# Attention and mixture-of-experts block on one core: queries and keys projected transposed, heads placed by DMAs

## What is computed

```python
xn = layernorm(x)
# latent branch, 16 heads: 16 content + 64 rotary features each
c_q, c_kv = xn @ w_dq.T, xn @ w_dkv.T
q = concat([heads(c_q @ w_uq.T), rope(heads(c_q @ w_qr.T))])
k = concat([heads(c_kv @ w_uk.T), rope(heads(xn @ w_kr.T))])
v = heads(c_kv @ w_uv.T)
s = softmax(causal(q @ k.T / sqrt(80))) @ v @ w_out.T
# second branch, 16 heads of 16
xr = rmsnorm(xn, w_ln1)
h = softmax(causal((xr @ Wq.T) @ (xr @ Wk.T).T / 4)) @ (xr @ Wv.T)
x2 = xn + h @ Wo.T
g = silu(x2 + top2_of_8_experts(rmsnorm(x2, w_ln2)))
out = x + s * g
```

## Time and profile before

| | us |
|---|---|
| median of three runs | 896.05 |
| the profiled execution's own time | 900.06 |
| its span, first to last instruction | 898.3 |
| TensorE matmul busy | 822.7 (92%) |
| VectorE busy | 612.4 (68%) |
| ScalarE busy | 502.1 (56%) |
| GpSimd busy | 391.4 (44%) |
| mean granted TensorE clock | 0.945 |

### The profile page before, as it was taken

One profiled execution on the slowest core, in us unless ns is written; L12 is line 12 of the kernel. 1 busy time (PEld: TensorE's weight loads), 2 busy tenths in 40 slices (PEclk: granted clock), 3 DMA queues, 4 the chain that ended last, 5 costly groups with the idle time before them and its releaser, 6 DMA issues.

```text
span 898.3 us, 18344 instructions
## 1 busy us (share of the span) xinstructions
PE 822.7 (92%) x6432; PEld 735.3 (82%) x6432; DVE 612.4 (68%) x2191; ACT 502.1 (56%) x1089; POOL 391.4 (44%) x538
## 2 busy tenths in 40 slices
PE   5889999999999999999999999988669999999980
PEld 3778988898897898888889889866459999999980
DVE  4976666767767676667776675762537878887854
ACT  2445466457347536536645744644237878787851
POOL 4632342344344344434434434414344565656640
PEclk9988999999999999999999999977769999999995
DMA  9000000000000000000000000122368999999836
GB/s 291 2 1 2 14 1 12 16 13 3 25 14 2 25 14 1 26 13 2 14 14 13 3 25 13 11 87 86 105 183 207 237 230 232 255 261 243 234 37 198
DMA packets 49871, 71.07 MB, mean 79 GB/s; under 512 B 12067, under 2 KB 36003, under 8 KB 49763
## 3 DMA queue, kind: packets, MB, share of 16 engines
q1 hardware_dynamic: 39060, 57.41, 20.8%
q0 software_dynamic: 9856, 12.13, 7.7%
q10 hardware_dynamic: 864, 0.36, 0.2%
HBM read 55.13 MB, written 14.81 MB: 78 GB/s over the span
## 4 chain that ended last, share of the span: by engine, by line
PE 76%; DVE 10%; ACT 5%; DMA 4%; issue 3%; POOL 1%; SPq 1%; POOLq 0%; ACTq 0%; DVEq 0%
PE ps L608 62%; PE ps L702 6%; PE ps L739 3%; DVE ps L1509 2%; ACT ex L1175 2%; DVE ps L1506 1%; PE ps L635 1%; DMA expert_rows<-yo,slot_of 1%; DMA ln<-in_w_ln 1%; PE ps L992 1%; PE ps L644 1%; DMA xg<-x_normalised,slot_of 1%; SPq L377 1%; DVE xr L1788 1%; DVE s_tok L1786 1%
## 5 line engine op out<-in xcount | busy, mean ns | idle before, releaser
L544 POOL TENSOR_SCALAR_AFFINE_SELECT ex<-ex 128x256 f32<-128x256 f32 x256 | 104.4, 411 | 232.1 <-ACT ex L1175 211.4
L608 PE MATMUL ps<-qt,kt 81*128 81x128 f32 (+2 forms) x768 | 166.6, 331 | 3.8 <-ACT ex L1175 2.0
L1175 ACT ACTIVATE ex<-ps 128x384 f32<-128x384 f32 x240 | 116.0, 492 | 95.0 <-PE ps L608 93.2
L522 POOL TENSOR_TENSOR ex<-ex 128x256 f32<-128x256 f32 x128 | 102.5, 801 | 110.3 <-DVE ex L1466 109.3
L1506 DVE CUSTOM_DVE_ANT_0 ps<-ps,mask 128x128 f32<-128x128 f32 x256 | 77.1, 301 | 92.2 <-PE ps L608 88.8
L608 PEld LDWEIGHTS ps<-qt,kt 81*128 81x128 f32 (+1 forms) x768 | 111.1, 197 | 15.8 <-issue 6.0
L1509 DVE CUSTOM_DVE_ANT_0 ps<-ps,mask 128x256 f32<-128x256 f32 x256 | 118.6, 463 | 0.0
L585 POOL DMA_INDIRECT expert_rows<-yo,slot_of x46 | 77.0, 1674 | 82.6 <-ACT yo L1310 55.1
L1347 DVE TENSOR_TENSOR wel<-raw,weh 128x768 fp32r<-128x768 f32 x92 | 87.7, 956 | 18.3 <-ACT weh L1045 18.3
L608 PE MATMUL ps<-wh,xth 128*128 128x320 f32 (+2 forms) x352 | 96.1, 355 | 4.4 <-DVE wl L1347 3.0
L1045 ACT ACTIVATE qt<-ps 80x512 f32<-80x512 f32 (+1 forms) x96 | 56.8, 592 | 61.5 <-PE ps L702 59.4
(11 more groups left out here) (160 smaller groups left out, 1914.3 us busy)
## 6 DMA issues: line engine op xcount, KB each, us to landing
raw<-in_w_experts SPq DMA_DIRECT2D x92, 384.0 KB, 4.5
mla_branch<-s_b SPq DMA_DIRECT2D x8, 256.0 KB, 2.1
expert_rows<-xn SPq DMA_DIRECT2D x8, 256.0 KB, 2.1
x_normalised<-otk SPq DMA_DIRECT2D x8, 256.0 KB, 2.1
xr<-in_x SPq DMA_DIRECT2D x1, 2048.0 KB, 10.4
s_tok<-mla_branch SPq DMA_DIRECT2D x4, 512.0 KB, 6.9
w_cols_raw<-in_w_cols SPq DMA_DIRECT2D x1, 1792.0 KB, 15.6
x<-expert_rows SPq DMA_DIRECT2D x3, 512.0 KB, 5.1
```

What stands on the lines that cost most here:

```text
L522: nc.gpsimd.tensor_tensor(t, t, swp[:, n % 2, :, :], ALU.add).then_inc(tokd, 1)
L544: nc.gpsimd.affine_select(a, a, [[0, 2], [1, P]], ALU.is_ge, zero, 0, -1).then_inc(exm, 1)
L608: return nc.tensor.matmul(o, a, m, start=start, stop=stop, skip_group_check=True, **k)
L1175: nc.scalar.activation(ex[:, h % (2 * G), :], ps[4 + h % 2][:, P:4 * P], ACT.Exp, scale=scale).then_inc(ex_, 1)
```

## The change

The projection of P1 is turned round: the weights are the stationary operand and all 256 tokens of a sequence the moving one, so a unit comes out with features on partitions and tokens along the free axis. There are 12 such units of 128x512 (content queries and keys `nq`, `nk`; rotary `q0` to `k3`, four heads each; the second branch's `mq`, `mk`) and one of values, in the order `UNITS`. The weights' columns are reordered on the host so that a unit's partitions are (feature, head) pairs. The TensorE transposes of P1 and all of P2 go away, with their evictions. In their place a unit is written to one of five staging slots `stg`, and DMAs on the SP queue move it into `qt`/`kt` (SBUF to SBUF, a feature's four heads from four partitions into one). The second branch's parts go from staging to a DRAM tensor `multi_heads` in 12 DMAs and come back into `qt2`/`kt2` in 8, four per half of the heads. Their scale, which ran along partitions before, is a row transposed by TensorE (`rms_rows`) into `rsb`. VectorE rounds the placed queries, ScalarE the placed keys, four heads at a time, each into a ring of three. The maxima's matmuls run two heads ahead of the scores; `max1`'s heads 0 and 1 stand in P1 after unit `k3`, `max2`'s at the start of a turn. `max_t1` moves to the end of T2. In the prologue the mean squares and the second branch's low weights come ahead of all rotary products.

```diff
+NS = 5
+RING = 3
+UNITS = ("nq", "nk", "q0", "k0", "q1", "k1", "q2", "k2", "q3", "k3", "mq", "mk", "v")
+BANK = dict(nq=0, nk=1, q0=4, k0=5, q1=0, k1=1, q2=4, k2=5, q3=0, k3=1, mq=4, mk=5, v=0)
+STAGED = dict(nq=1, nk=1, q0=2, k0=2, q1=2, k1=2, q2=2, k2=2, q3=2, k3=2, mqh=4, mql=2, mkh=4, mkl=2)
...
+            def place_content(b, a):
+                s, _, _ = place(b, ("nq", "nk")[a])
+                sp.wait_ge(nkd, 2 * b + a + 1)
+                sp.dma_start((qt, kt)[a][RD:HW, :, :], stg[:, s, :, :]).then_inc(sl[s], 16)
+
+            def place_rope(b, g, a):
+                s, _, _ = place(b, "qk"[a] + str(g))
+                sp.wait_ge(tokd, 8 * b + 2 * g + a + 1)
+                for t in range(2):
+                    o = (qt, kt)[a][t * RD // 2:(t + 1) * RD // 2, G * g:G * (g + 1), :]
+                    sp.dma_start(o, stg[:, s, t, :]).then_inc(sl[s], 16)
...
+            def store_mha(b, a):
+                for name, parts, ready in (((("mqh", (0, 1), hi2), ("mql", (2,), s2d)),
+                                            (("mkh", (0, 2), hi2), ("mkl", (1,), s2d)))[a]):
+                    s, _, _ = place(b, name)
+                    sp.wait_ge(ready, 2 * b + a + 1)
+                    for k in parts:
+                        for e in range(2):
+                            sp.dma_start(mha_d[a, e, D * k:D * (k + 1), :, :].rearrange("d (j t) s -> (d j) t s", t=2),
+                                         stg[e * ST:(e + 1) * ST, s, :, :]).then_inc(sl[s], 16)
+
+            def load_mha(b, t):
+                wait(sp, st2, 16 * (b - 1) + 8 * (t + 1))
+                for name in ("mqh", "mql", "mkh", "mkl"):
+                    s, _, done = place(b, name)
+                    sp.wait_ge(sl[s], done)
+                for e in range(2):
+                    for a, o, n in ((0, qt2[:, e, :, :], ST), (1, kt2, MROW2)):
+                        sp.dma_start(o[ST * e:ST * e + n, 4 * t:4 * (t + 1), :].bitcast(F32),
+                                     mha_d[a, e, 0:n, 4 * t:4 * (t + 1), :]).then_inc(mrd[t], 16)
...
-            for b in range(1, last):
-                row1(b)
-                keep_x2(b - 1)
-                store_x2(b - 1)
+            for b in range(last):
+                if b >= 1:
+                    keep_x2(b - 1)
+                    store_x2(b - 1)
                 row2(b)
-                store_s(b)
-            row1(last)
+                stage_p1(b + 1, lambda: store_s(b))
+                load_mha(b + 1, 0)
+                row1(b + 1)
+                load_mha(b + 1, 1)
...
+            def features(o, c0):
+
+                k = 0
+                for w, a in ((wh, xth), (wl, xth), (wh, xtl)):
+                    for e in range(ET):
+                        i = mm(o, w[:, e, c0:c0 + P], a[:, e, :], k == 0, k == 2 * 3 - 1)
+                        k += 1
+                return i
...
+                free = dict(q0=(ex1, 16 * b), k0=(ex1, 16 * b), q1=(nkd, 2 * b + 1), k1=(nkd, 2 * b + 2),
+                            q2=(roped, 8 * b + 1), k2=(roped, 8 * b + 2), q3=(roped, 8 * b + 3),
+                            k3=(roped, 8 * b + 4), mq=(roped, 8 * b + 5), mk=(roped, 8 * b + 6), v=(roped, 8 * b + 7))
...
-                    if h > 0:
-                        max_head(h - 1)
+                    if h + 2 < H:
+                        max_head(h + 2)
+                    if h == H - 1:
+                        tail()
...
                 if more:
+                    max2(b)(0)
+                    max2(b)(1)
+                    if not first:
+                        to_tokens()
...
+                    p1_with_m1(b + 1, {"nq": after_first, "k0": between, "k1": back, "k2": project})
+                    stage_t2(b, max1(b + 1), {5: lambda: project_v2(b + 1)})
...
+            def rounded_k(b, g):
+
+                landed(b, "nk")
+                landed(b, "k" + str(g))
+                wait(act, m1d, G * (NG * b + g - RING + 1))
+                copy(kr[0:HW, (NG * b + g) % RING, :, :], kt[0:HW, G * g:G * (g + 1), :]).then_inc(rkd, 1)
...
+                keep_content(b, 0)
+                keep_content(b, 1)
+                if b >= 2:
+                    gate_exp(b - 2)
+                if b > 0:
+                    keep_back(b - 1, fb1, of1, o1)
+                else:
+                    rms_rows(b)
+                for g in range(RING):
+                    rounded_k(b, g)
+                mha_high(b, 0)
+                mha_high(b, 1)
...
+            def products(b, n):
+
+                name = "qk"[n % 2] + str(n // 2)
+                s, free, _ = place(b, name)
+                wait(dve, sl[s], free)
+                if n == 0:
+                    wait(dve, pv1, NG * b)
+                wait(dve, tokd, 8 * b + n - 1)
+                dve.wait_ge(p1d, unit(b, name))
+                a = of_unit(name)
+                nc.vector.tensor_tensor(stg[:, s, :, :], a, cos_t[:, :].unsqueeze(1).broadcast_to([P, 2, S]), ALU.mult)
+                nc.vector.tensor_tensor(prb[:, n % 2, :, :], a[:, ::-1, :], sin_t[:, :, :], ALU.mult).then_inc(roped, 1)
...
             def stage_p1(b, after):
...
+                for n in range(2 * NG):
+                    products(b, n)
                     after.get(n, lambda: None)()
...
+                    if n == 5:
+                        rounded_q(b, 0)
+                rounded_q(b, 1)
+                first_m1(b)
+                mha_scale(b, 0)
+                mha_scale(b, 1)
+                mha_low(b, 0)
+                mha_low(b, 1)
+                rounded_q(b, 2)
...
-                for h in range(H):
+                for h in range(2, H):
+                    if h == 6:
+                        rounded_q(b, 3)
                     maxima(b, h, h, negm1, m1d, mx1)
...
+            mean_squares()
+            mha_weights_low(0)
+            mha_weights_low(1)
+            stage_p1(0, {n: lambda n=n: normalised_two(n + 1) for n in range(7)})
```

More of the change, by code:

```diff
@@ L84, with unit, place @@
 C_OWN = C_THR
+def unit(b, name):
+    return len(UNITS) * b + UNITS.index(name) + 1
+def place(b, name):
+    n = len(STAGED) * b + list(STAGED).index(name)
+    counts = list(STAGED.values()) * (b + 1)
+    free = 16 * sum(counts[n % NS:n:NS])
+    return n % NS, free, free + 16 * counts[n]
 def wait(engine, semaphore, value):
@@ L593, in _ @@
                 scatter(blk)
-        def order(step_proj, step_tr, after):
-            for i in range(2 * 9 + 2):
-                if i < 18:
-                    step_proj(i)
-                if i >= 2 and (i - 2) % 9 != 8:
-                    step_tr(i - 2, 8 * ((i - 2) // 9) + (i - 2) % 9)
-                after.get(i, lambda: None)()
         @block.tensor
@@ L743, in raw_scores, with max_t1 @@
+            def max_t1(b):
+                wait(pe, roped, 8 * b + 8)
+                max_t(b, ps[1], negm1, mx1, mtr1)
             def raw_scores(o, q, k):
@@ L853, in before_h0 @@
                     wait(pe, v2d, b + 1)
+                    wait(pe, m2p, 2 * (b + 1) + 2)
                 heads(b, scores2, st2, ex2, exm2, pv2, ov2, v2, before_h0, lambda: wait(pe, sd, b + 1), max_head,
[L855 to L860 removed]
+                      lambda: max_t1(b + 1), after)()
             def route_transpose(r):
                 wait(pe, xb2d, r + 1)
[L865 removed]
+                wait(pe, mte1, min(r + 2, B))
                 for e in range(ET):
@@ L1126, in qk2_high, with landed @@
[L1126 to L1133 removed]
+            def landed(b, name):
+                s, _, done = place(b, name)
+                act.wait_ge(sl[s], done)
@@ new lines, in landed, with rounded_q @@
+            def landed(b, name):
+                s, _, done = place(b, name)
+                dve.wait_ge(sl[s], done)
+            def rounded_q(b, g):
+                landed(b, "nq")
+                landed(b, "q" + str(g))
+                wait(dve, m1d, G * (NG * b + g - RING + 1))
+                copy(qr[0:HW, (NG * b + g) % RING, :, :], qt[0:HW, G * g:G * (g + 1), :]).then_inc(rrd, 1)
+            def stage_p1(b, after):
+                for n in range(2 * NG):
+                    products(b, n)
+                    after.get(n, lambda: None)()
+                    if n == 5:
[7 more added lines that the diff above has]
+                rounded_q(b, 2)
```

582 lines of the change are left out of this document (264 added, 318 removed).

## The result

The changed kernel takes 868.81 us (median of 4 runs, 866.15 to 876.8) against 897.07 for the kernel before on the same chip: ratio 0.9697, 95% interval 0.9627 to 0.9767. So it is faster, by 28 us, where 90 were forecast, and it lies outside the range of 788 to 845. The profiled execution has a span of 868.1 us, against 898.3 before.

What follows compares the result with a forecast made beforehand. TensorE was taken to bound the turn almost throughout. A turn of 24.2 + 12.1 + 3.2 + 21.2 = 60.7 against 72.3 saves 81.2 over seven, the prologue 8.9: 896.05 - 90.1 = 806 us, own range 797 to 818, overall 788 to 845.

Steps and rivals of the forecast that it cites:

- P1: Projection stage of a turn: only the transposes go, leaving 24.2 us against 28.3.
- rival (e): P1: projections with 256-column matmuls are not as fast as in T2, 0.01 us more each, 12 us more; chance 0.05.
- the cover of 3 us: P1: waits for banks, staging slots and placements cost nothing, each covered by 3 us; later landings cost the difference.
- T2 becomes VectorE's: T2: VectorE's queue of maxima sets its length, as TensorE needs only 0.47 per head; 12.1 us against 17.57.
- off the path: P1 and T2: ScalarE's key roundings replace its sixteen evictions and delay nothing, as the ring lets them run ahead.
- The stall of 2.0: Turn's start: TensorE waits 2.0 us for the first half of `qt2`/`kt2` out of DRAM.
- (a): Turn's start: the loads are there in time, no stall, 7 x 2.0 less, 792 us; chance 0.14.
- (b): Store and load chain: SP issues cost 0.90 each, the stall is 7.6, 39 us more, 845; chance 0.18.
- (d): Whole turn: the one SP queue becomes the bound, from 1.2 us an issue on; about 955 us, slower; chance 0.05.
- Rival (c), the clock: T2 and the turn's start: TensorE falls to half clock after waits, 2.5 us each turn, 823 us; chance 0.16.
- T1: Stage T1: loses two max2 heads at 0.42, gains a 0.4 wait for the normalisation; 21.2 us against 21.6.
- 14 normalisations 4.5: Prologue: VectorE's 14 normalisations take 4.5 us of the 62 at which its queue ends, ahead of T1(0).

Runs made afterwards that it cites:

- e1_fill: Changed kernel plus matmuls nobody reads on TensorE, 24 and 28 in the two waits ahead of the first T1 and 12 in each T2; 855.48 us, ratio 0.954.
- e2_k2_later: Changed kernel with ScalarE making the second branch's high parts ahead of rounding the third group of latent keys, not behind it; 863.49 us, ratio 0.964.
- e9_keys_last: Changed kernel with three banks of maxima, third key group rounded later, and query loads issued before the key stores are waited for; 850.67 us, ratio 0.951.
- e6_six_stores: Changed kernel with the second branch's twelve stores of 128 KB made six of 256 KB; 1066.6 us, ratio 1.187.

## Why the prediction was wrong, step by step

- **P1 held.** 24.2 forecast, 24.0 and 24.1 in the two turns whose clock stayed up. Projections of 256 columns cost what they cost elsewhere; rival (e) is out. VectorE waited for staging slots 0.9 us in all the turns, so the cover of 3 us was enough, though the rotary units' placements land in 3.7 to 3.9 us and not in 3.
- **T2 failed: "TensorE needs only 0.47 per head and would be done earlier, so T2 becomes VectorE's."** The step took T2 as VectorE's queue alone. But its TensorE also has the projected values (1.42) and `values` (0.79 a group) in between, and with two banks neither engine can work ahead through the other's pause. The 14 maxima and a rounding are 9.0 us of VectorE's work. On average over the seven T2 they took 13.6 us: 11.9 in e1_fill, whose T2 all run at full clock (+2.9), and 1.7 more that go with the lower clock. They started 2.5 us into T2 and not 1.2 (+1.3): the queue was costed for VectorE only, without ScalarE's queue between high and low parts, in which "off the path" was said of the very roundings that stood there. Behind the last maximum came 2.3 us and not 1.9 (+0.4), 0.3 of it the loads' wait. This is 6.3 of T2's 6.4.
- **The start.** The forecast has the loads' chain end 14.0 us into T2; in the three turns where TensorE waits for it, T2 is 17.8 to 18.9 us long. An issue of a store is 0.63, not 0.55 (12 in 7.55), which is 1.0 for twelve. The first store goes out 0.55 us into T2(3) and 0.96 into T2(2), and not 0.6 ahead; SyncE waited for its high part only 1.0 us in two turns, and moving that part ahead of the rounding (e2_k2_later) left it at 0.56, so what holds it back is what stands in front of it in the queue: the placements of `k3` and `store_s`, which the chain's sum left out. The last load was in use 6.4 us behind the start of its issue in T2(3), and the forecast has 4.6. It took landing times from a kernel whose DMA engines were 4% busy; here they are 71% busy in T2(3). That the one comes from the other is likely, but no run shows it. The stall of 2.0 is there, but hidden under the late maxima: forecast and measurement have two chains of 14 and 12, and of about 18 both. Rivals (a) and (b) are both out as reasons, and (d), which was the side of slower, never came near: issues of 0.63 are far from its 1.2. (Its 955 was a slip besides: 19.4 us a turn more than forecast, seven times, on 806 is 942.)
- **The landing time.** By the fixed cost and the rate that the prediction took from the Trainium skill's page "DMA: Bandwidth & Descriptors", section "Anatomy of one DMA", the loads would land in an estimated 2.4 and 2.6 us. That section is about DMAs that GpSimd issues, and these are SyncE's; their medians are 5.0 us (`kt`, 192 KB) and 4.8 us (`qt`, 256 KB), so the measurement decides against it.
- **Rival (c), the clock, came true**, at about its price of 2.5 us a turn: T1 22.5 on average against 22.0 at full clock, P1 24.75 against 24.1, and up to 1.8 in T2 (18.2 against 16.4 in e1_fill). It came on top of the failed step and not in its place. I gave it 0.16 as a case by itself, where it should have been joined to every case that leaves TensorE waiting.
- **T1** at full clock is 22.0, not 21.2: the term is mis-sized by 0.8, 5 us in all. TensorE is idle for 0.98 us of T1(3), where it was 0.22.
- **The prologue failed too, in three steps.** First, "14 normalisations 4.5". VectorE's queue began as forecast (33.1) and its last maximum was done at 72.1, not at 64. Of these 8.1 us the normalisations are 6.8: the seven pairs took 11.3 us. In the kernel before they stood one at a time between products; here they come in pairs, and GpSimd's sum, now 1.4 us and not 0.8, begins beside the first of a pair. The normalisations before and after (minimum, median and maximum in ns), and one pair:

```profile
L350 DVE TENSOR_SCALAR xn<-xn,mv,rstd x14: 396/400/404, 33.6 to 51.6; 128x256 f32<-128x256 f32 x14
L370 DVE TENSOR_SCALAR xn<-xn,mv,rstd x14: 396/877/1389, 34.3 to 52.1; 128x256 f32<-128x256 f32 x14
42.79 1.70 DVE L370 TENSOR_SCALAR xn<-xn,mv,rstd 128x256 f32<-128x256 f32 x2
42.95 1.39 POOL L599 TENSOR_TENSOR stg<-stg,ex 128x512 f32<-128x512 f32 x1 [1.43 <-DVE ex L1540]
44.41 0.68 DVE L1539 TENSOR_TENSOR stg<-ps,cos_t 128x512 f32<-128x512 f32 x1
```

  The second of the pair ends when GpSimd's sum does. That one held up the other is read from this; no run has them apart. (TensorE's wait of 6.19 us at the first maxima is a wait for VectorE's rounding, so it is this same queue and no further term.) Second, the 4.5 us from the last maximum to T1(0) were 9.7: TensorE waits there 3.58 for the loads and 4.17 for the row. The row DMA was costed for a turn (behind one half of the loads) and not for the prologue's own order (behind both). Together this is the 13.4 us of T1(0)'s start. Third, T1(0) at half clock was not in the sum. It cost 11.7 us (52.6 against the 40.9 of e1_fill); the table shows only 7.1 of it because the forecast's 45.4, an average turn, was 4.5 too much for the first, which has no turn before it to finish.

None of the signs that the prediction named for being wrong came up: in the loop TensorE did not wait in P1 for `roped` or a slot, and no wait at the start of a turn was above 1.5 us. None of them watched T2's maxima, where the miss was.

What stays open: why T2 of e9_keys_last has hardly a wait for the loads, when its last load is issued hardly sooner than in the changed kernel (the issue ends 12.1 us into T2(3), against 12.3) but lands within 4.2 us of that, where it takes 5.8 in the changed kernel and 5.0 in e1_fill. Fewer DMAs in flight at that moment would explain it; no run tells it apart.

## What to carry to other kernels

When two engines hand results back and forth through two buffers, a stage costs the longer of them only if neither has other work in between; otherwise add the pauses. A third buffer alone did not remove them here (12.0 us of maxima, as with two); three banks and the longest pause moved to an earlier place brought them to 10.5, against 9.0 of pure work. Follow every queue that a chain passes through, since a wait that is harmless for its own result (a rounding that runs ahead) delays whatever stands behind it. And look for the second chain that ends at the same point: here cures for the first alone gave 2 to 5 us, and with the second chain's order changed too, 18.

## What the runs showed of the hardware

TensorE stayed at half clock for 41 us in one piece while its records show it busy throughout the last 25 (matmuls of 81 and 80 rows with 128 and 256 columns among projections; the waits of 3.58 and 4.17 us lie in its first 16 us); with 52 unread matmuls in these waits (e1_fill) it was at half for 10 us only, and T2(0) came 9.7 us sooner. A store of 256 KB with a slowest dimension of 2 held the issuing queue 3.4 us on average (e6_six_stores), more than five times as long as a store of 128 KB with a slowest dimension of 64 (0.63, changed kernel). And a VectorE operation that reads and writes SBUF took 0.40 us in the kernel before, and up to 1.39 in the changed kernel, as the second of a pair beside GpSimd's sum of 1.4 us.
